# A two-layer relational network whose stages no longer meet at barriers

## The reference, cut to what matters

```
h = maximum(layernorm(x), 0)
x = x + L0(h, ...)                      # four layers of attention and MLP
h = maximum(layernorm(x), 0)
x = x + L1(h, ...)                      # the two relational layers:

def rgcn_gate_layer(x, row, col, edge_type, basis, att, gate_w, root, bias):
    w = einsum('rb,bio->rio', att, basis)           # one matrix per relation, 2 relations
    x_j = x[col]
    msgs = [(sigmoid(x_j @ gate_w[r,:,0])[:, None] * x_j) @ w[r] for r in (0, 1)]
    agg = segment_sum(where(edge_type == 0, msgs[0], msgs[1]), row)
    return agg + x @ root + bias
h   = relu(rgcn_gate_layer(x, ..., layer 1))
out =      rgcn_gate_layer(h, ..., layer 2)
```

## Time and profile before

| | us |
|---|---|
| median of 3 runs (lowest, highest) | 2596.27 (2594.19, 2598.52) |
| the profiled execution, its own time | 2591.04 |
| its span, first to last instruction | 2589.2 |
| PE busy in the span | 2355.8 (91%) |
| DVE busy | 1654.6 (64%) |
| ACT busy | 1134.9 (44%) |
| POOL busy | 529.0 (20%) |
| mean granted TensorE clock | 0.971 of full |

### The profile page before, as it was taken

How to read it: one execution, slowest core, us unless ns; L and a number is a source line. 1 busy time by engine, 2 the same in 40 slices (tenths; PEclk the granted TensorE clock), 3 DMA queues, 4 the chain that set the end, 5 groups by cost and what they waited for, 6 DMA issues and landing times.

```text
span 2589.2 us, 36524 instructions
## 1 busy us (share of the span) xinstructions
PE 2355.8 (91%) x13669; PEld 1981.9 (77%) x13669; DVE 1654.6 (64%) x3648; ACT 1134.9 (44%) x1794; POOL 529.0 (20%) x397
## 2 busy tenths in 40 slices
PE   4989996698999998999999999999999977897989
PEld 1665553388998897998888998888899866776867
DVE  7589994555887754787754787764787735343233
ACT  2216662324775323776233776333677312231221
POOL 1200000002663001664000665000565000000000
PEclk9999998799999999999999999999999988998999
DMA  8836669711103101101211110311110223132023
GB/s 182 223 87 137 133 141 255 219 55 48 40 21 97 57 27 48 40 20 62 85 35 47 29 32 34 107 31 36 40 40 3 72 65 116 41 112 77 15 74 103
DMA packets 62256, 199.78 MB, mean 77 GB/s; under 512 B 6794, under 2 KB 7242, under 8 KB 58250
## 3 DMA queue, kind: packets, MB, share of 16 engines
q1 hardware_dynamic: 57124, 188.18, 26.7%
q10 hardware_dynamic: 4966, 9.32, 1.2%
HBM read 160.27 MB, written 37.19 MB: 76 GB/s over the span
## 4 chain that ended last, share of the span: by engine, by line
PE 76%; DVE 8%; DMA 6%; ACT 4%; issue 4%; SPq 1%; POOL 0%; ACTq 0%; DVEq 0%
PE PS L1017 9%; PE PS L1045 8%; PE PS L799 6%; PE PS L953 6%; PE PS L954 6%; PE PS L955 6%; PE PS L1031 5%; PE PS L939 4%; PE PS L850 4%; PE PS L943 4%; PE PS L940 4%; DMA basis_t<-in_L_gnn_basis_dram 4%; PE PS L1186 4%; PE PS L1197 4%; PE PS L831 2%
## 5 line engine op out<-in xcount | busy, mean ns | idle before, releaser
L775 POOL TENSOR_SCALAR prob<-prob,inv_den 125x1000 f32<-125x1000 f32 x160 | 444.4, 2777 | 0.0
L799 PE MATMUL PS<-basis_t,att_z 120*128 120x512 f32 x512 | 256.1, 621 | 46.5 <-DMA basis_t<-in_L_gnn_basis_dram 46.4
L763 POOL TENSOR_TENSOR rstd<-var_eps,neg_half 125x2 f32<-125x2 f32 x45 | 32.5, 722 | 1126.7 <-DVE var_eps L1540 1126.7
L1367 ACT ACTIVATE prob<-prob,neg_max 125x1254 f32<-125x1254 f32 x160 | 215.5, 1347 | 72.5 <-DVE neg_max L1846 72.5
L1841 DVE CUSTOM_DVE_ANT_0 prob<-PS,sbias 125x1254 f32<-125x1254 f32 x160 | 233.0, 1456 | 8.8 <-issue 5.9
L1045 PE MATMUL PS<-pT_hi,v_hi 125*128 125x250 f32 x800 | 236.2, 295 | 0.0
L1860 DVE TENSOR_TENSOR pT_lo<-PS,pT_hi 125x1000 fp32r<-125x1000 f32 x160 | 191.0, 1194 | 52.5 <-ACT pT_hi L1384 52.5
L1045 PE MATMUL PS<-pT_lo,v_hi 125*128 125x250 f32 x800 | 223.9, 280 | 0.0
L1045 PE MATMUL PS<-pT_hi,v_lo 125*128 125x250 f32 x800 | 222.7, 278 | 0.0
L1031 PE MATMUL PS<-ident,prob 125*125 125x125 f32 x1600 | 201.1, 273 | 7.1 <-DVE pT_lo L1863 7.1
L1031 PEld LDWEIGHTS PS<-ident,prob 125*125 125x125 f32 x1600 | 196.0, 188 | 13.8 <-issue 9.1
(11 more groups left out here) (310 smaller groups left out, 5785.7 us busy)
## 6 DMA issues: line engine op xcount, KB each, us to landing
basis_t<-in_L_gnn_basis_dram SPq DMA_DIRECT2D x32, 1920.0 KB, 13.4
sbias<-score_bias SPq DMA_DIRECT2D x40, 548.6 KB
adj<-adj SPq DMA_DIRECT2D x20, 546.9 KB
w_lo_raw<-in_L_gnn_m_w_dram SPq DMA_DIRECT2D x8, 1024.0 KB, 6.5
score_bias<-cnt SPq DMA_DIRECT2D x10, 548.6 KB
adj<-count_t SPq DMA_DIRECT2D x10, 546.9 KB
xc<-x_lat SPq DMA_DIRECT2D x12, 448.0 KB
x_first<-x_lat SPq DMA_DIRECT2D x10, 448.0 KB
```

Of the source, the lines that this page charges most:

```text
L775: pool.tensor_scalar(prob[u % 3][:, 0:SPLIT], prob[u % 3][:, 0:SPLIT], inv_den[0:T, u % 4:u % 4 + 1], None, ALU.mult)\
L799: g = pe.matmul(PS[:, 6 + n % 2, :], att_z[n // (NW // 2)][:, 15 - row:143 - row], basis_t[load % 3][:, q, :], start=(row == 0), stop=(row ...
L1367: act.activation(prob[u % 3][:], prob[u % 3][:], ACT.Exp, bias=neg_max[0:T, u % 4:u % 4 + 1], scale=SCALE, accum_out=den[0:T, u % 4:u % 4 ...
```

## The change

- The four barriers go: pe_end and its like, r_end, and the wait for the stored h_rgcn.
- The stage before prepares the next one. In the last MLP, SP loads the three matrices of the first relational layer into the buffers of wk, wv and wq, the five pairs of x into buffers of their own (xr), the first counts, and both bias rows. ScalarE and VectorE split the matrices where a layer before the last splits those of its successor. VectorE's node_moments(p) adds x, takes the moments and writes the bias nmr of the norm; ScalarE's node_input(p) applies norm and relu in one pass into self_term. It runs one pair behind the MLP; the last pair comes after it. TensorE turns pair 0 before the last second_layer. The sum x is stored to x_lat by SP, and the output of the last MLP is no longer stored and read back.
- The counts of the first two aggregation tiles are loaded and widened during the node products (pairs 1 and 3). Each later load, adj(n + 2), is issued after adj_lo of n.
- The second layer's three matrices are loaded at once when the first layer's node products are done, and split at t = 3, 5, 7.
- The first layer's output stays in self_term, tile for tile. TensorE turns its first pair after the ninth of the ten aggregation tiles.
- Gates go to one PSUM bank (1), products to banks 2 to 4, transposes to 6 and 7, aggregations to 5 and 0. The halves of the gate weights are made once, ahead of the four layers. Loads and stores of pairs are split at row 112 (ROWS).

The core of the diff:

```diff
-        wr_hi = [m(f"wr_hi{i}", [128, 4, D], f32r) for i in range(3)]
-        wr_lo = [m(f"wr_lo{i}", [128, 4, D], f32r) for i in range(3)]
-        w_rawr = m("w_rawr", [128, 4, D])
+        wr_hi, wr_lo, wr_raw = (wk_hi, wv_hi, wq_hi), (wk_lo, wv_lo, wq_lo), (wk_raw, wv_raw, wq_raw)
+        m = Map(SCRATCH + 6 * 4 * 4 * D)
+        rb_raw = [m(f"rb_raw{l}", [1, D]) for l in range(2)]
+        R_T = m.at
+        rT_hi, rT_lo = [], []
+        for i in range(2):
+            rT_hi.append(m(f"rT_hi{i}", [128, 4, W], f32r))
+            rT_lo.append(m(f"rT_lo{i}", [128, 4, W], f32r))
+        m = Map(R_T)
+        xr = [m(f"xr{p}", [T, 2, D]) for p in range(3)]
+        m = Map(R_T)
+        xres = [m(f"xres{i}", [T, D]) for i in range(2)]
+        m = Map(R_T + 2 * 4 * 4 * W)
+        adj_lo = m("adj_lo", [T, NB, T], f32r)
...
+                if last:
+                    load_r(0, 0)
+                else:
                     load_w(lay + 1, wk, wk_raw, 0)
...
+                wait(sp, w_hi_done, lay, W1)
+                if last:
+                    for p in range(3):
+                        load_input(p)
+                    load_r(0, 1)
+                    wait(sp, wo_ps, lay, 2 * NP - 1)
+                    load_r(0, 2)
+                    load_input(4)
+                    load_adj(0)
+                    for p in range(NP):
+                        sp.wait_ge(r_x1_ready, p + 1)
+                        for r0, r1 in ROWS:
+                            sp.dma_start(pair_rows(x_lat, p)[r0:r1, :, :], xr[p][r0:r1, :, :]).then_inc(x_stored[p].sem, 16)
+                        if p == 0:
+                            load_input(3)
+                        if p == 1:
+                            for l, bias in enumerate((bias1, bias2)):
+                                sp.dma_start(rb_raw[l][:], bias.rearrange("(a n) -> a n", a=1)).then_inc(r_small_in, 16)
+                    continue
+                load_w(lay + 1, wv, wv_raw, 1)
...
-            for s in (pe_end, act_end, dve_end, pool_end):
-                sp.wait_ge(s.sem, 1)
             for p in range(NP):
                 wait(sp, x_stored[p], "final", -1)
...
+            sp.wait_ge(r_h_ready, NP)
+            load_adj(1)
+            for l in range(2):
+                sp.wait_ge(r_mm_ps, 3 * NT * (l + 1))
+                if l == 0:
+                    for n in range(3):
...
+                    if n + 2 < 2 * NT:
+                        sp.wait_ge(r_adj_lo, n + 1)
+                        load_adj(n + 2)
...
+                        else:
+                            wait(pe, yT_lo_done, lay, mlp_y(NP - 1, a))
+                            turn_nodes(0, 0, a)
...
+                    if l == 0 and t == NT - 2:
+                        for a in range(2):
+                            turn_nodes(1, 0, a)
...
+            def node_input(p):
+
+                s = NORMS.index(("final", p)) % 4
+                act.wait_ge(r_moments, p + 1)
+                for a in range(2):
+                    h = act.activation(self_term[:, 2 * p + a, :], xr[p][:, a, :], ACT.Relu, bias=nmr[0:T, s, a:a + 1],
+                                       scale=rstd[0:T, s, a:a + 1])
+                h.then_inc(r_h_ready, 1)
 
...
+                    if p == 1:
+                        adj_high(NT * l)
+                    if p == 3:
+                        if l == 0:
+                            wait(act, x_stored[3], LAYERS - 1, 0)
+                        adj_high(NT * l + 1)
...
+            def node_moments(p):
+
+                norm = ("final", p)
+                n = NORMS.index(norm)
+                wait(v, x_done, LAYERS - 1, 2 * p + 1)
+                v.wait_ge(r_x_in[p], 32)
+                v.tensor_tensor(xr[p][:], xr[p][:], x_c[p][:], ALU.add).then_inc(r_x1_ready, 1)
+                v.wait_ge(r_x1_ready, p + 1)
+                norm_stats(xr[p], *norm)
+                v.wait_ge(rstd_ready.sem, n + 1)
+                v.scalar_tensor_tensor(nmr[0:T, n % 4, :], mv[0:T, n % 4, 0:4:2], -1.0, rstd[0:T, n % 4, :],
+                                       ALU.mult, ALU.mult).then_inc(r_moments, 1)
...
+                    if last_layer and p:
+                        node_moments(p - 1)
+                    elif p in (1, 2):
+                        next_norm(p - 1)
+                    if p == 1:
+                        w_low(wv_hi, wv_lo, wv_raw, lay, 7)
+                    elif p == 3:
+                        w_low(wq_hi, wq_lo, wq_raw, lay, 8)
+                    elif p == 4 and last_layer:
+                        bias_row(0)
                     for a in range(2):
                         add_mlp(p, a)
-            v.drain().then_inc(dve_end.sem, 1)
-
-
...
-                def normalise(p):
-
-                    x, y = xr[p % 2], yr[p % 2]
-                    v.wait_ge(r_x_in[p % 2], 32 * (p // 2 + 1))
-                    v.tensor_tensor(x[:], x[:], lr[p % 2][:], ALU.add).then_inc(r_x1_ready, 1)
-                    v.wait_ge(r_x1_ready, p + 1)
-                    norm_stats(x, "final", p)
-                    if p >= 2:
-                        v.wait_ge(r_hT_ps, 2 * (p - 1))
-                    norm_apply(x, y, "final", p)
-                    v.tensor_scalar(y[:], y[:], 0.0, None, ALU.max).then_inc(r_h_ready, 1)
...
+                v.wait_ge(r_mm_ps, 3 * NT * (l + 1))
...
-                    link(v.tensor_tensor(res[t % 2][:], PS[0:T, t % 2, :], self_term[:, t, :], ALU.add))
+                    x = self_term[:, t, :]
+                    link(v.tensor_tensor(x, PS[0:T, AGG_BANK[t % 2], :], x, ALU.add))
                     if l == 0:
-                        v.tensor_scalar(res[t % 2][:], res[t % 2][:], 0.0, None, ALU.max).then_inc(r_res_ready, 1)
+                        v.tensor_scalar(x, x, 0.0, None, ALU.max).then_inc(r_res_ready, 1)
+                        if t == 0:
+                            bias_row(1)
                         if t in SPLIT_AT:
-                            weights_low(1, SPLIT_AT.index(t))
+                            w = SPLIT_AT.index(t)
+                            w_low(wr_hi[w], wr_lo[w], wr_raw[w], "final", w)
```

More of the change, by code:

```diff
@@ L69, in gnn_kernel @@
         gate_sb = sb("gate_sb", [128, 2, R])
+        gw_hl = [sb(f"gw_hl{l}", [128, 4, 2 * R], f32r) for l in range(2)]
+        nmr = sb("nmr", [128, 4, 2])
         large = sb("large", [1, 1])
@@ L596, in _ @@
                 load_x(1, x_c[1])
-                if not last:
+                if last:
+                    load_r(0, 0)
+                else:
                     load_w(lay + 1, wk, wk_raw, 0)
@@ L609, in _ @@
                             .then_inc(x_stored[p].sem, 16)
-                    if p == 0 and not last:
+                    if p == 0:
                         wait(sp, wo_ps, lay, 2 * NP - 1)
@@ L776, in _ @@
                         .then_inc(normed.sem, 1)
-                for norm in NORMS:
-                    if norm[0] == lay and norm[1] != "attention":
-                        inv_std(*norm)
-            pool.drain().then_inc(pool_end.sem, 1)
-            for p in range(NP):
-                inv_std("final", p)
+                first = NORMS.index((lay, "mlp", 0))
+                for norm in NORMS[first:NORMS.index((lay + 1, "attention", 2)) if lay + 1 < LAYERS else len(NORMS)]:
+                    inv_std(*norm)
         @block.tensor
@@ L1488, in _, with adj_high @@
+                    if last and p:
+                        node_input(p - 1)
+            def adj_high(n):
+                act.wait_ge(r_adj_in[n % 2], 32 * (n // 2 + 1))
+                if n >= 2:
+                    act.wait_ge(r_agg_ps, n - 1)
+                act.activation(adj_hi[n % 2][:], adj16[n % 2][:], ACT.Copy).then_inc(r_adj_hi, 1)
+            for l in range(2):
                 for p in range(NP):
@@ L2019, in _ @@
                 for p in range(NP):
-                    if l == 0 and p + 1 < NP:
-                        normalise(p + 1)
                     for a in range(2):
```

330 lines of the change are left out of this document (121 added, 209 removed).

## The result

| | changed | before |
|---|---|---|
| median of 4 runs, us | 2522.47 (2519.68 to 2525.23) | 2595.23 (2592.42 to 2598.52) |
| profiled execution, us | 2519.68 | 2591.04 |
| its span, us | 2517.6 | 2589.2 |
| ratio | 0.9719, 95% interval 0.9707 to 0.9730 | 1 |

72.8 us less, or 2.8%. The forecast was 2520, with a range of 2511 to 2537. It was close for the right main reason, and one of its steps failed.

A forecast was written before the change was run, and what follows sets the result against it. TensorE bounds it up to 2118 us; then idle and slow clock between three-pass products can go. From 2117.86, 1.8 + 0.9 + 1.5 + 98.1 + 92.95 + 0.9 + 2.0 + 98.1 + 92.95 + 5.8 = 395.0 against 471.3: median 2520, range 2511 to 2537.

The forecast's parts named there:

- Last MLP +1.8 and turn +0.9: Last MLP: VectorE's added preparation costs 1.8 us (0 to 6), and turning pair 0 there costs TensorE 0.9.
- The rival that the MLP pays in full: Last MLP: VectorE's 24.6 us of new work falls wholly on TensorE's path instead of 3.3; 2541 us, chance 0.12.
- Idle before the gates 1.5: Start of first node products: TensorE idles 1.5 us (0 to 6) waiting for VectorE's bias row.
- The flag's load: Before the first gates: the count flag's load comes onto TensorE's path, taken as 0 us, upper end 2.
- Aggregations 92.95 each: Both layers' aggregations: 92.95 us each at full clock, without the barrier, load and slow start.
- Change of layers 2.0: Between the layers: VectorE's add, relu, low half and hand-overs leave 2.0 us (1.8 to 4).
- Third count tile at 15.5: Aggregation: behind three matrices, the counts land near 15.5 us into the stage, needed at 16.3; slack 0.8, cost 0.
- Node stages 98.1 each: Both layers' node products: 98.1 us each at full clock, without slow gates and slow first products.
- What the two kinds of stage cost at full clock: Aggregation and node stages: long idle stretches are paid twice through slow clock; without it 92.95 and 98.1 us.
- The rival: Queue and clock: third count tile 5 us late, slow starts of 2.0 and twice 3.6 behind idles; 2534, chance 0.15.
- the forecast's own conditions: Wrong if third-tile idle exceeds 2 us, clock hits 0.5 after 2118, MLP grows over 6, or node stage exceeds 101.
- a granted clock of 0.61 over 53 us: 53 us behind the last MLP: clock 0.61, read as half of TensorE's 19.6 busy us at 1.2 GHz.

The follow-up runs named there:

- e_inputs: Changed kernel with only the first layer's input arithmetic (sums, moments, norm, relu, first turn) and bias row put back behind the last MLP; median 2531.95 us.
- e_bias: Changed kernel with only the first bias row formed one node pair earlier on VectorE; median 2521.67 us.
- e_counts: Changed kernel with each layer's first two count tiles loaded and widened only after its node products; median 2540.47 us.
- e_queue: Changed kernel with an unread 2.56 MB memory copy issued on SP behind the second layer's matrices, ahead of the third count tile; median 2529.78 us.
- e_both: Changed kernel with the first bias row one pair earlier and the second layer's first low halves made before the last aggregation wait; median 2515.83 us.
- e_fill: Changed kernel with unread full-width products, 6 behind the last MLP and 8 behind layer 1's last aggregation, waits kept; median 2520.26 us.

## Why the prediction was right, and its one wrong step

The steps in their order, forecast and measured:

- Last MLP +1.8 and turn +0.9: from the issue of the load of x_second to TensorE's end 98.96 us (2020.76 to 2119.72), against 96.63; e_inputs puts the whole at 2.3. Right, 0.4 too high. The rival that the MLP pays in full is out.
- Idle before the gates 1.5, for the bias row: 1.45, for the bias row. The flag's load costs nothing that shows: in e_bias the gates follow with no idle.
- Aggregations 92.95 each: 93.2 and 93.2, from the first product to VectorE's last add, the turn's 0.9 in the first taken off. Neither idles at its start; e_counts shows the 16.5 us that this is worth.
- Change of layers 2.0: 1.83, VectorE's chain of add, relu and low half.
- Third count tile at 15.5: 14.6. In the order of the queue, and e_queue shows the slack.
- Node stages 98.1 each: 99.96 and 101.58. This is the step that failed: "What the two kinds of stage cost at full clock" tied the slow clock to long idle stretches, on the strength of one row with 2.7 us of scattered idle at 1.00. A single idle of 1.45 or 1.83 us was enough, and cost 1.65 and 3.24. e_both, e_fill and the eight stages without an idle show it. The sum at full clock was right: 98.3 where 98.1 was forecast.

Those two are 4.9 us, about the 4.7 by which the span came out over the forecast (2517.6 for 2512.9). The rival had given slow starts to these idles, at 3.6 each, but only together with a count tile that came late. They are separate mechanisms and should have been two rivals; its clock half happened at 4.9 of 7.2, its queue half not. By the forecast's own conditions (clock at 0.5 after 2118, a node stage over 101 us) it was wrong in that point, though the time came out in its range: the profiled execution is 5.0 over its forecast of 2514.7, and the median lies 2.8 above it and not 5.2 as before, which gave half of that back by luck. One reading of the prediction was loose: a granted clock of 0.61 over 53 us is the lower level for about four fifths of them, (1 - 0.61) / 0.5, and not for half. Nothing in the sum rests on it.

## What to carry to other kernels

Take barriers and what stands behind them apart: here the barriers put back alone cost 4.7 us, and the loads, splits and round trips behind them, put back one by one, over 40 in sum, so a prepared input pays where a removed wait doesn't. Look for the last short waits of TensorE too: 1.45 and 1.83 us cost 0 to 1.8 times their length again in slow clock, and moving two small VectorE pieces ahead of a wait closed both for nothing. And look at the shape of each transfer before restructuring: splitting 125 rows into 112 and 13 gave 10 us of the old kernel's time and 1 us of the new one's tail.

## What the runs showed of the hardware

- The slow stretch behind a short idle comes in sizes (0, about 1.7, about 3.3 us) that differ between executions with the same idle to 0.01 us. With the gap closed or filled with products there was none in eight stages. An idle of 0.72 us ahead of 20 products of 512 columns brought none either time (4.93 us for them, 4.82 without it).
- Behind an idle of 5 to 7 us the next 20 products of 512 columns took 6.6 to 6.7 us in all three cases, instead of 4.8.
- A 125-row store of one result (256 KB) took a microsecond longer than the same in 112 and 13 rows. The DMA share was 0.32 in it and 0.94 in the split one; in loads of pairs 0.33 and 1.07.
- 2.56 MB copied within memory delayed the next transfer of its queue by 7.0 us.
